# Last batch's rows prepared behind the first shared units, a cast divided between ScalarE and VectorE, and fewer GpSimd pauses, in an attention and mixture-of-experts kernel

## The reference

```python
q, k, v = (x @ W.T + b).reshape(16, 256, 16 heads, 8)      # three of them
attn = softmax(q k^T / sqrt(8)) * head_mask
x1 = layernorm(x + (attn v) @ Wo.T + bo)                   # 4096 tokens x 128
shared = gelu(x1 @ Wfc_s + bfc_s) @ Wproj_s + bproj_s      # 128 -> 512 -> 128
probs = softmax(x1 @ Wr);  take the best 2 of 8 experts, their weights normalised to 1
routed = sum over the two of gate * (gelu(x1 @ Wfc[e] + bfc[e]) @ Wproj[e] + bproj[e])
out = layernorm(x1 + shared + routed)
```

## Time and profile before

| what | value |
|---|---|
| median of 3 runs | 517.42 us (516.01 to 517.75) |
| the profiled execution's own time | 517.43 us |
| its span, first to last instruction | 515.7 us |
| granted TensorE clock, mean | 0.929 |
| busy: PE, DVE, ACT, POOL | 421.4, 364.3, 330.7, 317.8 us |
| attention, until the second block begins | 0 to about 285.4 us |
| shared expert | to about 340 us |
| routed experts | to about 468 us |
| from POOL's last send to the end | 484.6 to 515.7 us |

### The profile page before, as it was taken

The page is one execution under the profiler, slowest core; times in us unless marked ns, Lnnn a source line. Parts: engine busy times, 40 slices in busy tenths (PEclk is TensorE's granted clock), DMA queues, the critical chain, the costliest instruction groups (busy, mean ns, idle before and its releaser), DMA issues. The chain is left out here.

```text
span 515.7 us, 13682 instructions
## 1 busy us (share of the span) xinstructions
PE 421.4 (82%) x4871; PEld 279.6 (54%) x4871; DVE 364.3 (71%) x768; ACT 330.7 (64%) x625; POOL 317.8 (62%) x421
## 2 busy tenths in 40 slices
PE   4999999999999999999781699798999999991000
PEld 2434555554555555545441366577999999991000
DVE  4367888788878878788582369767787777775381
ACT  1127888787887888887440799645667767770252
POOL 4322478667373758575427576667678787877651
PEclk9999999999999999999797799898999999997555
DMA  3222553546434565531001112432371111117231
GB/s 87 73 63 74 157 156 108 142 111 162 124 105 136 147 177 156 146 84 45 23 27 36 62 43 58 126 110 65 99 215 48 47 45 43 48 30 267 81 117 54
DMA packets 63125, 50.25 MB, mean 97 GB/s; under 512 B 7354, under 2 KB 54596, under 8 KB 63060
## 3 DMA queue, kind: packets, MB, share of 16 engines
q1 hardware_dynamic: 58516, 40.91, 27.9%
q0 software_dynamic: 4544, 8.47, 5.2%
HBM read 24.96 MB, written 22.95 MB: 93 GB/s over the span
## 5 line engine op out<-in xcount | busy, mean ns | idle before, releaser
L563 DVE TENSOR_REDUCE row_max<-s_ps 128x2 f32<-128x512 f32 x256 | 164.8, 683 | 47.5 <-PE s_ps L708 45.6
L417 ACT ACTIVATE probs<-ring_ps 128x1024 f32<-128x1024 f32 x128 | 130.9, 1023 | 45.9 <-PE ring_ps L726 45.4
L1513 POOL DMA_INDIRECT results<-gated,rows_in x78 | 90.7, 1163 | 25.7 <-issue 23.2
L1350 POOL DMA_INDIRECT slots<-rows,slot_at x64 | 67.0, 1047 | 37.9 <-issue 17.1
L708 PE MATMUL s_ps<-qk_stack 24*128 24x256 f16 x512 | 83.4, 270 | 7.7 <-DVE row_max L563 2.6
L1665 ACT ACTIVATE hid<-h_ps,bias 128x256 f32<-128x256 f32 x156 | 61.2, 475 | 42.4 <-PE h_ps L1599 42.4
L726 PE MATMUL ring_ps<-qk_stack 26*128 26x256 f16 x512 | 84.2, 274 | 0.0
L744 PE MATMUL av_ps<-probs,v_aug 128*32 128x256 f32 x1024 | 68.5, 385 | 0.0
L708 PEld LDWEIGHTS s_ps<-qk_stack 24*128 24x128 f16 x512 | 33.8, 92 | 62.0 <-issue 32.0
L1617 PE MATMUL y_ps<-w,hid 128*128 x312 | 57.8, 221 | 0.0
L1618 PE MATMUL y_ps<-w,hid 128*128 x312 | 57.6, 220 | 0.0
(11 more groups left out here) (221 smaller groups left out, 944.2 us busy)
## 6 DMA issues: line engine op xcount, KB each, us to landing
qk_stack<-qk_rows SPq DMA_DIRECT2D x64, 96.0 KB
slots<-empty_row SPq DMA_DIRECT2D x13, 390.0 KB, 5.2
qk_rows<-qk_parts SPq DMA_DIRECT2D x16, 256.0 KB, 2.6
rows<-results SPq DMA_DIRECT2D x8, 512.0 KB, 6.9
rows_in<-slots SPq DMA_DIRECT2D x3, 1040.0 KB, 7.5
w_stage<-in_w_fc SPq DMA_DIRECT2D x9, 256.0 KB, 3.2
w_stage<-in_w_proj SPq DMA_DIRECT2D x9, 256.0 KB, 3.6
x_t<-in_x_t SPq DMA_DIRECT2D x16, 128.0 KB, 2.2
```

The lines of the kernel that those rows point to most:

```text
L417: nc.scalar.activation(probs[:, n % PROBS], ring(key), ACT.Exp, scale=SCORE_SCALE).then_inc(ring_emptied, 1)
L563: nc.vector.tensor_reduce(row_max[:, h], s1_ps[:, h % 2], AX_X, ALU.max, negate=True).then_inc(max_done, 1)
L1350: nc.gpsimd.indirect_dma_start(out=a["slots"][:, :], out_offset=bass.IndirectOffsetOnAxis(ap=a["slot_at"][:, k, tile:tile + 1], axis=0), i ...
L1513: nc.gpsimd.indirect_dma_start(out=a["results"][:, :], out_offset=bass.IndirectOffsetOnAxis(ap=rows_in[:, 2 * n + half, DEST:DEST + 1].bit ...
```

## The change

- The last batch leaves the attention block. At step 19 POOL no longer scales (`make_x1` is skipped for batch 15), DVE no longer makes x1 of it, and ACT's `take_high` and DVE's `take_low` of the last group are gone from the block's end. The second block begins on POOL with `find_scale` for batch 15, on DVE with `scale_rows` and `take_low`, and on ACT `take_high` stands behind unit 0.
- PE begins the second block with units 0 to 2; the turn of the last group follows unit 2, its logits unit 4, the counts unit 12 (before: ahead of unit 0, behind unit 1, behind unit 10). DVE's router steps stand some two units later, most of all the tables.
- POOL's sends in the attention block go from 9 to 5, and 59 remain for the second block. `PAUSE_EVERY` goes from 8 to 16.
- At step 17 the counts are taken one pair earlier on PE and ACT, and DVE's `gate`, `tally` and `level` stand ahead of `invert_sums` and `normalise`, `lay_out` and the rest where they were.
- `halve` of a routed block: columns 0 to 511 of the high half are made by ACT (`first_high`, a Copy with scale), columns 512 to 1023 by DVE with a tensor_tensor against a broadcast column `x_unit` in place of the tensor_scalar over all 1024. The low half waits for both.

```diff
-PLACED = {18: (2, 5), 19: (0, 2)}
+PLACED = {18: (3, 2)}
-Q_AT, K_AT, TURN_AT, LOGIT_AT, COUNT_AT = 0, 3, 2, 6, 3
+Q_AT, K_AT, TURN_AT, LOGIT_AT, COUNT_AT = 0, 3, 2, 6, 2
...
-PAUSE_EVERY = 8
+PAUSE_EVERY = 16
...
-                if gone.exists():
+                if gone.exists() and gone.n != BATCHES - 1:
                     make_x1(gone)
...
-            take_high(GROUPS - 1)
...
-            take_low(GROUPS - 1)
...
         @block.gpsimd
         def _(pool):
+            find_scale(nc, pool, a, Batch(BATCHES - 1))
             nc.gpsimd.memset(minus_half2[:], -0.5).then_inc(half_made, 1)
...
-            turn_rows(nc, pe, a, turned16, LAST_GROUP).then_inc(rows_turned, 1)
             pe.wait_ge(a["weights_low"], 2 * ALL + 2)
             for i in range(UNITS + SHARED_LAG):
                 if i < UNITS:
                     shared_fc(i)
-                if i == 1:
+                if i == TURN_UNIT:
+                    turn_rows(nc, pe, a, turned16, LAST_GROUP).then_inc(rows_turned, 1)
+                if i == LOGIT_UNIT:
...
+            def first_high(n):
+                act.wait_ge(projected, TOKEN_TILES + n - 3 if n >= 4 else TOKEN_TILES - GROUP * (1 - n // 2))
+                act.wait_ge(activated, UNITS + n + 1)
+                nc.scalar.activation(block_half(n, 0)[:, 0:FIRST], hid[:, block_cols(n)][:, 0:FIRST], ACT.Copy, scale=X_UNIT)\
+                  .then_inc(first_made, 1)
...
                 if n < SLOT_BLOCKS:
                     unit(n)
+                    first_high(n)
                 if n >= WEIGH_LAG:
                     weigh(n - WEIGH_LAG)
...
-                nc.vector.tensor_scalar(high, whole, X_UNIT, 1.0, ALU.mult, ALU.mult).then_inc(hidden_high, 1)
+                rest = CHUNKS * BLOCK - FIRST
+                nc.vector.tensor_tensor(high[:, FIRST:], whole[:, FIRST:], x_unit[:].to_broadcast([P, rest]), ALU.mult).then_inc(hidden_high, 1)
                 dve.wait_ge(hidden_high, UNITS + n + 1)
+                dve.wait_ge(first_made, n + 1)
```

More of the change, by code:

```diff
@@ L344, in make_x1 @@
             def make_x1(b):
[L346 to L351, removed]
+                find_scale(nc, pool, a, b)
                 if b.n not in BY_VECTOR:
                     pool.wait_ge(scale_done, 2 * b.n + 2)
-                for t in range(TILES):
-                    if b.n not in BY_VECTOR:
+                    for t in range(TILES):
                         nc.gpsimd.tensor_scalar(x1_all[:, b.n * TILES + t], z[:, t], mean_var[:, t, 0:1], rstd[:, t:t + 1],
@@ L527, in step @@
                     exp_pair(late, 7)
[L529 to L532, removed]
             act.wait_ge(consts_made, 2)
@@ L596, in take_mean @@
                     nc.vector.bn_aggr(mean_var[:, t], stats[:, t]).then_inc(stats_done, 1)
[L598 to L609, removed]
             router = Router(nc, dve, a)
@@ L644, in step @@
                     router.place(0, 1)
+                if t == ROUTE_STEP:
+                    router.gate(0)
+                    counts_taken(0)
+                    router.tally(0)
+                    router.level()
                 if last.exists():
@@ L651, in step @@
                 if t == ROUTE_STEP:
[L652 to L655, removed]
                     router.lay_out()
@@ L1097, in cut_rows, with find_scale, scale_rows, take_high @@
     nc.gpsimd.tensor_tensor(parts[:, tiles, D:2 * D], a["x1_all"][:, tiles], parts[:, tiles, 0:D], ALU.subtract)\
+      .then_inc(a["x_low"], 1)
+def find_scale(nc, pool, a, b):
+    pool.wait_ge(a["stats_done"], 4 * b.n + 4)
+    if b.n >= 1:
+        pool.wait_ge(a["x1_made"], 2 * b.n)
+    nc.gpsimd.tensor_scalar(a["var_eps"][:], a["mean_var"][:, :, 1], EPS, X_UNIT ** -2, ALU.add, ALU.mult).then_inc(a["scale_done"], 1)
+    pool.wait_ge(a["scale_done"], 2 * b.n + 1)
+    nc.gpsimd.tensor_tensor(a["rstd"][:], a["var_eps"][:], a["minus_half"][:], ALU.pow).then_inc(a["scale_done"], 1)
+def scale_rows(nc, dve, a, b):
+    dve.wait_ge(a["scale_done"], 2 * b.n + 2)
+    for t in range(TILES):
+        nc.vector.tensor_scalar(a["x1_all"][:, b.n * TILES + t], a["z"][:, t], a["mean_var"][:, t, 0:1], a["rstd"][:, t:t + 1],
+                                ALU.subtract, ALU.mult).then_inc(a["x1_made"], 1)
+def take_high(nc, act, a, g):
+    tiles = slice(g * GROUP, (g + 1) * GROUP)
+    act.wait_ge(a["x1_made"], 4 * g + 4)
+    nc.scalar.activation(a["rows1"][:].bitcast(F16)[:, tiles, 0:D], a["x1_all"][:, tiles], ACT.Copy).then_inc(a["x_high"], 1)
+def take_low(nc, dve, a, g):
+    tiles = slice(g * GROUP, (g + 1) * GROUP)
+    parts = a["rows1"][:].bitcast(F16)
+    dve.wait_ge(a["x_high"], g + 1)
+    nc.vector.tensor_tensor(parts[:, tiles, D:2 * D], a["x1_all"][:, tiles], parts[:, tiles, 0:D], ALU.subtract)\
       .then_inc(a["x_low"], 1)
@@ L1690, in _ @@
               .then_inc(logits_taken, 1)
-            for i in range(2, COUNT_UNIT - 1):
+            for i in range(LOGIT_UNIT + 1, COUNT_UNIT - 1):
                 shared_unit(i)
@@ L1842, in _ @@
             add(3)
+            shared_low(22)
+            make_table()
+            shared_low(23)
             finish_table()
-            for i in range(22, UNITS):
+            for i in range(24, UNITS):
                 shared_low(i)
```

79 lines of the change are left out of this document (44 added, 35 removed).

## The result

| | before | changed |
|---|---|---|
| time, median of 4 runs each | 517.13 us (516.01 to 517.75) | 511.38 us (508.5 to 513.05) |
| profiled execution: time, span | 517.43, 515.7 us | 512.18, 510.4 us |
| ratio to before, 95% interval | | 0.989 [0.986, 0.993] |

The change is 1.1% faster, by 5.7 us. The forecast was 494.4 us, a gain of 23, and its range began at 490 and ended at 502. The sign was right and the size four times too large.

What follows compares the result with a forecast made beforehand. POOL's sends bound the kernel: POOL would end at 461.6 us, 23.0 earlier (9.9 from the front, 13.1 from cheaper sends). Adding the 31.1 us tail gives a 492.7 span, 494.4 as time; 8-in-10 range 490 to 502.

Steps and rivals of the forecast that it cites:

- I take no cost; the bounds are 0 and the present 0.42 per block: Routed blocks: DVE's replacement tensor_tensor adds nothing to POOL's result sends, where each block's tensor_scalar had cost 0.42 us.
- My two overlaps: Sends near 314.43 and 403.02 on POOL, read as showing that DVE instructions with two SBUF inputs do not lengthen sends.
- Step 17 and the barrier: Attention block: first slot send 2.2 us earlier, at 265.7; POOL saves 7.4 us more; barrier opens at 275.8, not 285.4.
- Slot sends, pauses and landing: Behind the barrier: 59 sends 74.6 us, longer ones 2.2, three pauses 3.9, landing 2.19; first result send at 360.5.
- go with the tensor_scalar: Slot sends: of 5.6 us surplus over 64, some 3 fall into the routed stage and vanish with the tensor_scalar.
- Result sends: Routed blocks on POOL: 78 sends at 1.283 make 100.1 us, plus 1 for bias copies; POOL ends at 461.6.
- The supply: ACT's gated rows keep up: copy 0.63 us hidden, 0.15 us spare per block; last gated block done at 457.6.
- The ring of 8 holds 5.3 blocks of lag: Routed blocks: the ring of 8 buffers between ACT's gated rows and POOL's result sends holds the expected lag, 5.3 blocks.
- The tail: Final layernorm, from POOL's inversion of a root to the end of the span: stays 31.1 us.
- The first: Rival: routed tensor_tensor holds POOL as the tensor_scalar did; sends stay 1.464, POOL ends 474.7, time 507.5; chance 7%.
- The fourth: Rival: change does little, sends held by landing rather than issue and barrier set by another engine; 510 to 517; chance 3%.
- The third: Rival: ACT becomes a serial bound of the routed loop, period 3.70 us, time 520.7, slower than before; chance 3%.

## Why the prediction was wrong

**The step that failed** is the sentence "I take no cost; the bounds are 0 and the present 0.42 per block", and under it the belief that only the tensor_scalar held sends. The rows on record already spoke against it, had I read ends and not surpluses. The send of 403.02 ended at 404.42, 0.85 us behind the *end* of the tensor_scalar at 403.57. My two overlaps proved nothing: the send of 314.03 had begun 0.40 us before the scalar_tensor_tensor of 314.43, and the send of 404.73 began 0.11 us before the one of 403.61 ended at 404.84. Neither was a send that begins well beneath it. The trace of before has such sends, which the earlier trace rows don't show: six that began beneath a block's scalar_tensor_tensor took 1.55 to 1.67 us, ending 0.82 to 0.86 behind it. One of them:

```profile
388.75 1.22 DVE L1769 SCALAR_TENSOR_TENSOR hid<-hid 128x1024 f16<-128x1024 f32 x1
389.27 1.55 POOL L1513 DMA_INDIRECT results<-gated,rows_in  x1 [0.30 <-issue]
```

It ends at 390.82, 0.85 behind 389.97, and no tensor_scalar ran before 390.94. The second rule of the Trainium skill that I set aside (page "SBUF — State Buffer", section "Who interferes with whom", two SBUF inputs contend with a GpSimd instruction that reads SBUF) is what the runs show: 0.83 us behind the end with two SBUF inputs, 0.96 in all where the first of them is in PSUM. I had given it 7%.

**Why the divided cast was worth nothing.** The tensor_tensor takes the same 0.69 us as the tensor_scalar did and holds sends in the same way, so DVE's cover is unchanged: 0.69 + 1.23 us and their gap before (402.88 to 404.84) and in the changed kernel (386.59 to 388.61), some 2.0 us of a period of 2.98. The part left free, about 1.0 us, is shorter than the 1.28 from one send's start to the next, so of two sends at least one begins beneath a DVE instruction. Each block's pair then takes what the block takes: 1.40 + 0.98 + 0.60 before, 1.36 + 1.02 + 0.60 after, both 2.98. This is worked out from the rows; that the pairs are 2.98 in both is measured, where sends lie over routed blocks one after another.

By the steps of the forecast, where PSUM stands for the changed kernel with the gelu in PSUM:

| step | forecast | changed | PSUM |
|---|---|---|---|
| first slot send | 265.7 | 263.49 | 263.87 |
| POOL past the barrier | 275.8 | 276.06 | 273.84 |
| first result send | 360.5 | 366.52 | 358.39 |
| us per result send | 1.283, and 1 in all | 1.446 | 1.301 |
| last gated block done | 457.6 | 464.1 | 454.7 |
| POOL's last end | 461.6 | 479.33 | 459.86 |
| tail | 31.1 | 31.1 | 31.1 |

- *Step 17 and the barrier* were right together by luck. The first send was 2.2 us earlier than I took, and POOL gave that back in waiting 2.29 us for the moments of batch 14, a wait that the forecast had not.
- *Slot sends, pauses and landing* missed by 6.0 us at the first result send. I had let 3 us of surplus "go with the tensor_scalar"; instead, the sends over routed blocks were held there by the scalar_tensor_tensor. Five slot sends took 1.56 to 1.86 us (one such before), the 59 behind the barrier came out 7.1 us over 0.96 each where the sum had 2.5, and the wait for landing was 3.58 and not 2.19.
- *Result sends* missed by 11.7 us, 78 sends at 1.446 in place of 1.283 and 1 us. The two misses make the 17.7 us at POOL's last end (479.33 less 461.6), and with them the whole error of the profiled execution, 512.2 against 494.4.
- *The supply.* The last low half of the shared stage ended at 327.83, forecast 329.7. ACT's copy took 0.63 us and blocks went at 2.98, so ACT held, as forecast. "The ring of 8 holds 5.3 blocks of lag" failed with the sends: the first gated rows were made at 342.08 and sent from 366.52, 24.4 us, more than 8 blocks of 2.98.
- *The tail* was exact: 31.07 against 31.1.
- *The rivals.* The first had the right cause and too small a size (507.5), since it left the first result send at 360.5 and thought of the tensor_tensor alone. The fourth had the right band (510 to 517) by a wrong cause. The third, ACT as a serial bound, did not appear.

The forecast's own premise, sends held by nothing, gives 494.4 by its sum; where the experiment made the premise true in the routed loop, the kernel took 492.7, and no step of the PSUM column is over 3 us from the forecast. So the sum was sound to that, and the term that failed is the cost of a send over DVE's work: 0 in the forecast, the whole hold of before in the runs.

## What to carry to other kernels

When an engine looks slowed by another, line up the *end* of the slowed instruction with the ends of the other engine's instructions, and sort the cases by who began first: a constant distance (here 0.83 to 0.85 us) points to a hold that ends with the other's instruction, and an overlap in which the slowed one began first proves nothing. If GpSimd sends are the chain, count how long DVE runs in each period with two SBUF inputs, or with a tensor_scalar or cast from SBUF. Here the free part (1.0 us) was shorter than the step from send to send (1.28), and exchanging one holding instruction for another of the same length gave nothing; whether shortening or removing one alone would was not tried. Moving one input of all of them to PSUM freed the sends. Look for every instruction that shares the suspected cause before pricing the removal of one. A long stall (ACT's 14 us here) may be no more than a wait for the chain.

## What the runs showed of the hardware that I had not expected

- A tensor_tensor or scalar_tensor_tensor with two SBUF inputs, one of them even a broadcast column, holds an indirect send as a tensor_scalar or cast from SBUF does: the send ends 0.83 us behind it. The same instructions with the first input in PSUM hold nothing (0.96 us).
- Who begins first decides. A tensor_tensor that begins 0.12 us behind the send's start leaves it at 0.96. Two of the tensor_scalars, begun 0.28 us behind a send, still cost it 0.13 (1.09 at 41.64 above); no two-input instruction did so at that distance.
- ACT's gelu written over its own input in PSUM takes no longer: 1.54 us for four against 1.57 into SBUF, and its copy of 128x512 from PSUM 0.60 against 0.63:

```profile
354.85 1.54 ACT L1679 ACTIVATE h_ps<-h_ps,bias 128x256 f32<-128x256 f32 x4 [0.23 <-PE h_ps L1612]
356.48 0.60 ACT L1685 ACTIVATE hid<-h_ps 128x512 f16<-128x512 f32 x1
```

- DVE's tensor_scalar of 128x1024 takes 0.69 us from SBUF and 1.22 from PSUM. Its shorter time goes with the SBUF input, and so does its hold on POOL.
